# A fused transformer chain on one core: the key input of the FFN mixed before its product, squares on ScalarE, v copied between feature parts

## The reference, cut to what matters

```python
x = x + attn_a(layernorm(x))      # softmax attention, 16 heads, causal, ALiBi bias
x = x + ffn(layernorm(x))
x = x + attn_b(layernorm(x))      # linear attention with RoPE, features elu(.)+1, not causal
x = x + ffn(layernorm(x))         # the same weights

def ffn(x):
    x_prev = x shifted by one token
    xr = mu_r * x + (1 - mu_r) * x_prev
    xk = mu_k * x + (1 - mu_k) * x_prev
    r = sigmoid(xr @ W_r.T)
    k_act = square(relu(xk @ W_k.T))
    return r * (k_act @ W_v.T)

def attn_b(x):                    # per head; q, k, v = x @ w_qkv.T
    kv = k_feat.T @ v ; k_sum = sum(k_feat)
    out = (q_feat @ kv) / max(q_feat @ k_sum, 1e-6)
    return out @ w_out.T
```

## Time and profile before

| what | value |
|---|---|
| median of 3 runs | 388.31 us (388.29 to 397.62) |
| the profiled execution's own time | 385.37 us |
| its span | 383.0 us |
| busy PE / ACT / DVE / POOL | 342.7 / 293.9 / 147.3 / 40.2 us |
| mean granted clock of TensorE | 0.98 |

### The profile page before, as it was taken

How to read it: one execution, slowest core, us unless ns; L and a number is a source line. 1 busy time by engine, 2 the same in 40 slices (tenths; PEclk the granted TensorE clock), 3 DMA queues, 4 the chain that set the end, 5 groups by cost and what they waited for, 6 DMA issues and landing times.

```text
span 383.0 us, 6570 instructions
## 1 busy us (share of the span) xinstructions
PE 342.7 (89%) x2599; PEld 154.8 (40%) x2599; DVE 147.3 (38%) x399; ACT 293.9 (77%) x428; POOL 40.2 (10%) x57
## 2 busy tenths in 40 slices
PE   3988999999999899999998899999999988868795
PEld 1653333333223332232223232222222856868664
DVE  5731345214232322120303120210300779996965
ACT  1545556579999689999996799999999576983771
POOL 4500000000000000000000000000000253720340
PEclk9996899899999999999999999999999999999999
DMA  6475555520000000000000000000000300000002
GB/s 199 58 263 203 151 191 134 184 79 0 2 0 2 2 1 2 0 2 0 2 0 3 0 3 2 0 2 0 2 3 14 100 0 2 2 4 0 3 27 82
DMA packets 12019, 16.46 MB, mean 43 GB/s; under 512 B 945, under 2 KB 7473, under 8 KB 11825
## 3 DMA queue, kind: packets, MB, share of 16 engines
q1 hardware_dynamic: 11984, 16.00, 13.6%
HBM read 6.56 MB, written 2.62 MB: 24 GB/s over the span
## 4 chain that ended last, share of the span: by engine, by line
PE 57%; ACT 18%; DVE 10%; issue 9%; DMA 3%; SPq 1%; POOL 1%; DVEq 0%; ACTq 0%
PE ps L954 21%; PE ps L939 16%; ACT probs L451 13%; PE ps L794 7%; PE ps L963 3%; ACT x L451 3%; PE ps L846 3%; PE ps L999 2%; DMA kr<-probs 2%; PE ps L789 2%; DVE ot L653 2%; DVE probs L661 2%; DVE stats L526 1%; ACT scr L460 1%; DMA cs<-in_consts 1%
## 5 line engine op out<-in xcount | busy, mean ns | idle before, releaser
L451 ACT ACTIVATE probs<-ps 128x1024 f32<-128x1024 f32 (+6 forms) x222 | 170.4, 863 | 36.3 <-PE ps L939 35.4
L939 PE MATMUL ps<-qr,kr 38*128 38x512 f32 (+7 forms) x592 | 115.9, 435 | 4.5 <-ACT probs L451 4.1
L954 PE MATMUL ps<-probs,vaug 128*9 128x512 f32 (+6 forms) x888 | 98.9, 501 | 9.8 <-DVE probs L661 7.9
L939 PEld LDWEIGHTS ps<-qr,kr 38*128 38x128 f32 x592 | 51.5, 186 | 108.8 <-ACT probs L451 63.8
L451 ACT ACTIVATE x<-ps 128x1024 f32<-128x1024 f32 (+6 forms) x74 | 67.0, 957 | 6.6 <-PE ps L939 6.4
L661 DVE TENSOR_TENSOR probs<-probs,cs 128x512 f32<-128x512 f32 x60 | 41.0, 688 | 67.7 <-ACT probs L451 67.6
L653 DVE COPY ot<-ps 128x512 f32<-128x512 f32 x16 | 11.1, 691 | 135.5 <-PE ps L954 135.5
L380 POOL TENSOR_TENSOR rstd<-veps,neghalf 128x4 f32<-128x4 f32 x16 | 17.0, 1062 | 323.4 <-DVE veps L532 323.4
L794 PE MATMUL ps<-w,scr 128*128 128x128 f32 x288 | 35.9, 278 | 3.4 <-issue 3.1
L794 PEld LDWEIGHTS ps<-w,scr 128*128 128x128 f32 x288 | 33.9, 192 | 7.7 <-issue 5.8
L954 PE MATMUL ps<-x,vaug 128*9 128x512 f32 (+7 forms) x296 | 36.7, 541 | 0.0
(11 more groups left out here) (94 smaller groups left out, 217.9 us busy)
## 6 DMA issues: line engine op xcount, KB each, us to landing
x<-in_x SPq DMA_DIRECT2D x8, 256.0 KB, 4.2
qr<-parts_mid SPq DMA_DIRECT2D x16, 128.0 KB
kr<-parts_mid SPq DMA_DIRECT2D x16, 128.0 KB
qr<-probs SPq DMA_DIRECT2D x8, 128.0 KB
kr<-probs SPq DMA_DIRECT2D x8, 128.0 KB
qr<-parts_last SPq DMA_DIRECT2D x8, 128.0 KB
kr<-parts_last SPq DMA_DIRECT2D x8, 128.0 KB
out_y<-x SPq DMA_DIRECT2D x4, 256.0 KB, 2.3
```

The source lines that it names most:

```text
L451: nc.scalar.activation(slot[:, 2 * u:2 * u + 2, w0:w1], ps[:, b:b + 2, w0:w1], ACT.Exp).then_inc(exp_done, 1)
L939: ins = nc.tensor.matmul(ps[:, 2 * (n % 3) + v, w0:w1], kr[kb // TPC][a:a + ROWS, j, P * (kb % TPC):P * (kb % TPC + 1)], qr[unit.c][a:a + ...
L954: ins = nc.tensor.matmul(ps[32 * v:32 * v + V1, 6, w0:w1], vaug[:, kb, V1 * h:V1 * (h + 1)], probs_slot(unit)[:, v, w0:w1], start=(unit.i ...
```

## The change

1. The key input is mixed before the product: GpSimd writes prev_k = (1 - mu_k) * x_prev ahead of prev_r of the same chunk, VectorE adds mu_k * x to it (`mix_k_of`), and TensorE does one product with W_k. w_mu and its two VectorE instructions go; GpSimd waits once for 1 - mu.
2. relu(k) is squared on ScalarE (`Square`, SBUF to SBUF), right behind the relu; `k_squared` leaves VectorE.
3. On ScalarE, the copy of v of chunk n stands between the q and the k feature parts of chunk n; before, it stood behind both parts of chunk n + 1.
4. On TensorE, transposed q features and key-value sums of chunk n stand behind the v product of chunk n + 2; before, all four v products came first.

```diff
             def shift(f, n):
                 pool.wait_ge(xt_ready[(LN2, LN4)[f]], n + 1)
+                nc.gpsimd.tensor_scalar(prev_k[:, cols(n)], xt_f[:, cols(n)], omu[:, 1:2], 0.0, ALU.mult, ALU.add).then_inc(shifted_k, 1)
                 nc.gpsimd.tensor_scalar(prev_r[:, cols(n)], xt_f[:, cols(n)], omu[:, 0:1], 0.0, ALU.mult, ALU.add).then_inc(shifted, 1)
...
+            pool.wait_ge(mu_ready, 1)
             each(lambda n: shift_of(LN2, n), lambda n: shift(0, n))
...
                 nc.scalar.activation(relu_k[:, cols(n)], ps[:, high(n), :], ACT.Relu).then_inc(relu_ready, 1)
+                act.wait_ge(relu_ready, NCH * f + n + 1)
+                nc.scalar.activation(kact[:, cols(n)], relu_k[:, cols(n)], ACT.Square).then_inc(kact_ready, 1)
...
-            trail(lambda n: [feature_parts(s, n) for s in range(2)], take_v)
+            for n in range(NCH):
+                feature_parts(0, n)
+                take_v(n)
+                feature_parts(1, n)
...
-            nc.vector.tensor_scalar(w_mu[:, 0], w[:, W_KK:W_KK + D], w[:, MU_K:MU_K + 1], None, ALU.mult)
-            nc.vector.tensor_scalar(w_mu[:, 1], w[:, W_KK:W_KK + D], omu[:, 1:2], None, ALU.mult).then_inc(mu_ready, 1)
...
+            def mix_k_of(f, n):
+                dve.wait_ge(shifted_k, NCH * f + n + 1)
+                nc.vector.scalar_tensor_tensor(mix_k[:, cols(n)], xt_f[:, 1 + CH * n:1 + CH * (n + 1)], w[:, MU_K:MU_K + 1],
+                                               prev_k[:, cols(n)], ALU.mult, ALU.add).then_inc(mixed_k, 1)
...
-            def k_squared(f, n):
-                dve.wait_ge(relu_ready, NCH * f + n + 1)
-                nc.vector.scalar_tensor_tensor(kact[:, cols(n)], ps[:, high(n), :], 0.0, relu_k[:, cols(n)],
-                                               ALU.max, ALU.mult).then_inc(kact_ready, 1)
...
-            trail(lambda n: (mix_r(0, n), k_squared(0, n)), lambda n: add_mix(0, n, LN3))
+            trail(lambda n: (mix_k_of(0, n), mix_r(0, n)), lambda n: add_mix(0, n, LN3))
...
-            trail(lambda n: (mix_r(1, n), k_squared(1, n)), lambda n: add_mix(1, n, None))
+            trail(lambda n: (mix_k_of(1, n), mix_r(1, n)), lambda n: add_mix(1, n, None))
...
             def mix_k_in(f, n):
-                stage((xt_ready[(LN2, LN4)[f]], n + 1), ((y_added, y2_added)[f], n + 1))
-                pe.wait_ge(mu_ready, 1)
-                for i in range(2):
-                    ins = nc.tensor.matmul(ps[:, high(n), :], w_mu[:, i], xt_f[:, CH * n + 1 - i:CH * (n + 1) + 1 - i],
-                                           start=(i == 0), stop=(i == 1))
+                stage((mixed_k, NCH * f + n + 1), ((y_added, y2_added)[f], n + 1))
+                ins = nc.tensor.matmul(ps[:, high(n), :], w[:, W_KK:W_KK + D], mix_k[:, cols(n)], start=True, stop=True)
                 ins.then_inc(fk_psum, 1)
...
-            each(v_b, lambda n: (turn_q(n), summarize(n)),
-                 numerators)
+            in_turn(v_b, None, lambda n: (turn_q(n), summarize(n)))
+            each(numerators)
```

More of the change, by code:

```diff
@@ L137, in program @@
         kvb = scr[:, 15 * T + CH:15 * T + CH + D + H]
-        w_mu = scr[:, 15 * T + 2 * CH:15 * T + 2 * CH + 2 * D].rearrange("p (i n) -> p i n", i=2)
         nmt = probs[:, 0:2 * P].rearrange("p (a q) -> p a q", a=2)
@@ L175, in program @@
         att_psum, att_ready, y_psum, y_added = sems("att_psum att_ready y_psum y_added")
-        mu_ready, shifted, mixed, fk_psum, fr_psum, relu_ready, gate_ready, kact_ready, fv_psum, f_added = sems(
-            "mu_ready shifted mixed fk_psum fr_psum relu_ready gate_ready kact_ready fv_psum f_added")
+        mu_ready, shifted_k, shifted, mixed_k, mixed, fk_psum, fr_psum, relu_ready, gate_ready, kact_ready, fv_psum, f_added = sems(
+            "mu_ready shifted_k shifted mixed_k mixed fk_psum fr_psum relu_ready gate_ready kact_ready fv_psum f_added")
         bq_psum, bk_psum, bv_psum, rot_parts_q, rot_parts_k, bv_ready, rot_ready, rot_last, feat_act, feat_ready, qft_psum, qft_ready, kv_psum, kv_ready = sems(
@@ L687, in _ @@
             dve.wait_ge(w_rest, 16)
-            nc.vector.tensor_scalar(omu[:, :], w[:, MU_R:MU_K + 1], -1.0, 1.0, ALU.mult, ALU.add).then_inc(dve_step, 1)
-            steps[0] += 1
-            dve.wait_ge(dve_step, steps[0])
+            nc.vector.tensor_scalar(omu[:, :], w[:, MU_R:MU_K + 1], -1.0, 1.0, ALU.mult, ALU.add).then_inc(mu_ready, 1)
             nc.vector.memset(vb[:, :, D:D + 1], 1.0)
             nc.vector.memset(xt_f[:, 0:1], 0.0)
-            nc.vector.tensor_scalar(w_mu[:, 0], w[:, W_KK:W_KK + D], w[:, MU_K:MU_K + 1], None, ALU.mult)
-            nc.vector.tensor_scalar(w_mu[:, 1], w[:, W_KK:W_KK + D], omu[:, 1:2], None, ALU.mult).then_inc(mu_ready, 1)
             normalize(NCH, 0)
```

## The result

The changed kernel takes 415.6 us as the median of 4 runs (410.85 to 445.06), the kernel before 391.24 in the runs beside it: 1.061 times as long, 95% interval 1.047 to 1.075. The profiled execution took 413.37 us with a span of 411.6, 28.6 over the 383.0 of before. Executions of either kernel differ by several us through where TensorE's clock happens to fall, so ratios are of undisturbed runs and causes are read from stretches of the trace.

A forecast was written before the change was run, and what follows sets the result against it. It took TensorE to bound the FFNs before, then late k inputs and a loop through VectorE. Terms 10.7 + 1.8 + 7.4 = 19.9 us, plus 4 for the clock, gave 388.3 + 24 = 412.3 us, range 401 to 427.

The forecast's parts named there:

- the sum at full clock: Both FFNs and the feature stage together, without clock falls: 10.7 + 1.8 + 7.4 = 19.9 us later.
- the clock's term: TensorE at half clock for k product 0 and a transpose in each FFN, and one more such pair: +4 us.
- Start of the first FFN: First FFN, chunk 0: k product waits for GpSimd's prev_k and VectorE's mix, starting 5.84 us later, at 312.13.
- First FFN at full clock: First FFN: late start and a loop through add_mix and mix_k, rounds of 6.6 us; everything behind 10.7 us later.
- the walk: Following each engine's order with trace durations through the stages from the first FFN on: 19.9 us later at full clock.
- Feature part: Linear attention's features: ScalarE waits for v 0 after only q of chunk 0; last key-value sum 1.8 us later.
- Second FFN at full clock: Second FFN: k product 0 starts 3.8 us later, loop rounds of 5.25 us; last add_mix ends 7.4 us later.
- rival (a): Both FFNs: TensorE at low clock throughout, 38 us over before, 426 us; chance 0.20.
- SBUF shared between GpSimd and VectorE: Both FFNs: mixes and shifts take turns, costing about 0.5 us at each change, 1 to 2 us per FFN.
- (b): Both FFNs: only the starts are late and the loop does not close; 6.2 us over before, 394.5; chance 0.10.
- (c): Both FFNs: TensorE stays the bound and GpSimd's lateness is absorbed; 6.9 us saved, 381.4 us; chance 0.05.
- (d): ScalarE in both FFNs: Square needs another table, two loads per square, 20.6 us more, 433 us; chance 0.05.

The follow-up runs named there:

- kernel with fillers: The changed kernel with bf16 filler products on TensorE in its gaps, where it waits for mix_k; spans 405.3 and 406.5 us.
- the copy alone: The kernel before with only v copied between the q and k feature parts, TensorE's order as before; spans 384.7 and 386.2 us.
- the run with VectorE's order opened: The changed kernel with the mixes of chunk n + 2 ahead of add_mix of chunk n, in both FFNs; 1.027 times the time of before.
- the feature part alone: The kernel before with only the moved v copy and key-value sums two chunks behind v (parts 3 and 4); span 386.0 us.
- squares alone: The kernel before with only the squares moved to ScalarE (part 2), two k products kept; 1.007 times the time of before.

## Why the prediction was right

It gave 412.3 us, 24 over before, range 401 to 427. Measured: 415.6, which is 24.4 over the 391.24 of before, and 28.6 us between the two profiled spans. The mechanism is right and so is the sum at full clock (19.9 forecast, 20.0 measured). That the total came so near is partly luck: the clock's term was less than half of what the profiled execution lost to it, and the profiled execution of before had no fall of the clock behind 297 us at all. It was faster than most, while the forecast was set on a median 2.9 us slower. By the prediction's own steps:

- *Start of the first FFN, +5.84.* Measured 5.84, with GpSimd's shift, the mix of 1.17 us and TensorE's transposes behind the product, as written.
- *First FFN at full clock, +10.7.* The kernel with fillers has +10.8, and its k products 2 and 3 start within 0.3 us of where the walk put them, counted from the first mark. The round of 6.6 us is in the chain. The walk led the loop over ScalarE's order; TensorE's order holds it as well.
- *Feature part, +1.8.* 1.76 alone, with ScalarE waiting for v 0 as written, and the copy alone makes it.
- *Second FFN at full clock, +7.4.* Late start +3.82 (forecast 3.8), and from k product 0 to the end 20.3 us with fillers against 16.7 before: 7.4 in sum.
- *The clock, +4.* This term was mis-sized: 5.0 in the first FFN, 2.5 in the second, and 1.6 of the feature stage, 9.1. The two prices of the FFNs are differences between the changed kernel and the one with fillers, and the third is what is left of 3.3 beside 1.76, so that 10.8 + 1.8 + 7.4 + 9.1 gives the 29.1 measured is no proof of its own. I had let TensorE run slow for one product and transpose at each start and one more, and named a quick return at the start of the kernel. Rows 7 said otherwise: there the clock was down from 31.4 to 41.5 us with TensorE busy, and in the first FFN of the changed kernel it was down as long (310.1 to 320.3). It fell again in the first FFN's last round, in the second FFN, and around 361 us. The range up to rival (a) had allowed for it.
- *SBUF shared between GpSimd and VectorE.* mix_k took 1.17 us as the median of 8, and shifts up to 1.12 us when they took turns with mixes. The prediction's "0.26 us late" is not a row: it is 0.69 less the 0.43 of the wait. The mix of before starts at 310.91, some 0.05 us behind GpSimd's second shift, and a wait for the whole of that would be 0.63 us, not 0.43. So the rows show that the two engines take turns, but with a shorter wait than the prediction's reading gives from these starts. What this costs in all no run here prices by itself.
- Rival (a), low clock throughout, came true in part (mean clock 0.79 in the first FFN, 0.84 in the second). (b), the loop does not close, is out by the run with VectorE's order opened. (c), TensorE stays the bound, is out by its 22 us of waiting. (d), a table load for Square, is out by eight squares of 0.63 us and no load. The Trainium skill (ScalarE: Activation LUTs, "Table sets: the hidden batching unit") has cheap functions in every set and does not name Square; the trace shows it to run under the sigmoid table without a load.

## What to carry to other kernels

Halving a product on the busiest engine brings nothing if its input must first be made by engines that come to that work later: ask when the new input is ready, not what it costs. If an in-order engine gets a step that feeds the front of a pipeline, place it ahead of the steps that take from its end; here that alone gave back 14.4 of the 25.7 us that the FFNs had lost. A late first input is passed on to the end: here 2.1 us less of it gave 2.0. And count the gaps that such waits open on TensorE at its lower clock, together with the time until the clock is back, as a row of the same kernel shows it.

## What was not expected of the hardware

The same gap keeps the clock in one execution and loses it in another. Behind the exp table's load TensorE waits 2.4 to 2.9 us for ScalarE in all thirteen traces. Six of them kept 1.00, each with a gap of 2.41 us, among them before, the change and the feature part alone. Seven ran at half clock for 3.4 us soon after, among them squares alone and the v copy alone with the same 2.41 us. The first copy of v then came 15.9 to 16.5 us behind the load instead of 14.4 to 14.6. So a single trace can hold almost 2 us that its edit need not have made.

And SBUF-reading instructions in a row on two engines take turns: in the changed kernel from 384.87 us on VectorE's mixes took 1.17, 1.17 and 1.17 us and GpSimd's shifts 1.12 and 1.12, against 0.74 and 0.69 alone.
